# Rotary attention of a decoder's second layer: the product of the probabilities with the reciprocal sums moves from VectorE to GpSimd

## The chip, the cores and the metric

The kernel runs on one core of a Trainium2 chip. It is one program for a whole decoder of four layers (each with a self attention, a cross attention and a feed-forward part) on 32 sequences of 64 positions and width 128, all in fp32. The metric is the device time of one execution in microseconds, lower is better. The kernel before took 1555.16 us (median of 3 runs, 1553.07 to 1556.38).

In the profile's words PE is TensorE's matmul, PEld its weight load, DVE is VectorE, ACT is ScalarE, POOL is GpSimd and SP is SyncE.

## The reference

Only the self attention of layer 1 is touched. It has 16 heads of width 64, is causal, and turns queries and keys by a rotary table before their product:

```python
q, k = (apply_rope(q), apply_rope(k))
dots = jnp.einsum('bhid,bhjd->bhij', q, k) * scale
dots = jnp.where(causal, neg, dots)
attn = jax.nn.softmax(dots, axis=-1)
out = jnp.einsum('bhij,bhjd->bhid', attn, v)
out = out.transpose(0, 2, 1, 3).reshape(b, n, INNER)
out = jax.nn.relu(out @ W_o1) @ W_o2
```

After this comes a normalisation over the 128 features with a gain, and the sum is added to the stream `x`. The softmax's last step, the division by the row's sum of exponentials, is what the change moves.

## The kernel before

The 2048 tokens stand as 16 tiles of 128 rows (two sequences of 64). `rotary_attention` (from L1967) walks the tiles as a software pipeline that is written out by hand: each engine has its own loop over an index k, and in one turn of it works on several tiles at once, at different steps. The engines are tied by semaphores that count finished instructions, and each engine executes its own list strictly in order, so a wait holds back everything behind it.

Per tile t the steps are these.

- PE projects the queries into PSUM banks 0 and 1 and the keys into banks 2 and 3 (`project(t, 0)` and `project(t, 1)`, both L2018; the trace shows 16 matmul records for each), after the scores of tile t-1 have been read out of the same banks (`scored`, L2014).
- DVE multiplies each by the sine and the cosine table (`rotate`, L2205 and L2208). POOL adds the two products of the queries (L2192, two halves of 512), DVE those of the keys (L2217).
- PE multiplies queries and keys (`scores`, L2044).
- One turn later DVE adds the causal mask while it reads the scores from PSUM (`mask`, L2224), and finds the row maxima for the 16 heads (`find_max`, L2230 and L2232).
- ACT takes the exponentials head by head with their sums (`soften`, L2119; the sums land in `row_max`, 128x16).
- A further turn later DVE takes the reciprocals of the sums (L2238) and multiplies the 128x1024 probabilities by them, in place (L2240): the two instructions of `normalise`.
- PE turns the probabilities over (`turn_probs`, L2054), ACT copies them to SBUF (L2140), PE weighs the values (`weigh_values`, L2068), ACT copies the result (L2147), PE multiplies by the two output matrices (L2076 and L2083), with ACT's ReLU (L2151) and copy (L2127) between.
- DVE and POOL do the normalisations: statistics on DVE (L377, L380), the inverse root on POOL (`invert`, L387 and L389), and DVE applies it (L2256, L2259, L396).

PE's list in turn t is: `project(t,0)`, `turn_probs(t-2)`, `project(t,1)`, `weigh_values(t-2)`, half of the value projection of tile t+1 (L2031), `project_out(t-2)` (L2076), `scores(t)`, `project_mid(t-2)` (L2083), the other half of the value projection.

DVE's list in turn k is: `mask(k-1)`, `normalise(k-2)`, `find_max(k-1)`, `rotate(k,0)`, `rotate(k,1)`, the key sums, and then the normalisation steps of tiles k-4, k-5 and k-3.

POOL's list in turn k is: `invert` for tile k-5 and for tile k-4, then the query sums of tile k. In this stage POOL and SP issue no DMA inside the loop.

Of the kernel before, what the change touches and what calls it, by code (L numbers as in the profile page):

```python
# [13 lines left out]
ALU = mybir.AluOpType  # L14
# [5 lines left out]
B, S = 32, 64  # L20
NT = 16
# [178 lines left out]
def signals(core, names):  # L200


    words = names.split()
    turns = core.turns
    first = turns.taken
    turns.taken += len(words)
    return namedtuple("Signals", words)(*core.halves[turns.half][first:turns.taken])
# [112 lines left out]
def bcast(ap, dim, n):  # L320

    ap = ap.unsqueeze(dim)
    shape = list(ap.shape)
    shape[dim] = n
    return ap.to_broadcast(shape)
# [48 lines left out]
def measure(v, m, src, u, n=1):  # L374

    for t in range(u * n, u * n + n):
        v.bn_stats(m.stats_of[:, t], src[:, t]).then_inc(m.stats, 1)  # L377
    for t in range(u * n, u * n + n):
        v.wait_ge(m.stats, t + 1)
        v.bn_aggr(m.moments_of[:, t], m.stats_of[:, t]).then_inc(m.moments, 1)  # L380


def invert(c, g, m, u, n=1):

    own = slice(u * n, u * n + n)
    g.wait_ge(m.moments, u * n + n)
    g.tensor_scalar(m.var_eps_of[:, own], m.moments_of[:, own, 1], 1e-5, None, ALU.add).then_inc(m.var_eps, 1)  # L387
    g.wait_ge(m.var_eps, u + 1)
    g.tensor_tensor(m.rstd_of[:, own], m.var_eps_of[:, own], c.minus_half[:, 0:n], ALU.pow).then_inc(m.rstd, 1)  # L389


def scale(v, m, src, dst, u, n=1):

    v.wait_ge(m.rstd, u + 1)
    for t in range(u * n, u * n + n):
        v.tensor_scalar(dst[:, t], src[:, t], m.moments_of[:, t, 0:1], m.rstd_of[:, t:t + 1],  # L396
                        ALU.subtract, ALU.mult).then_inc(m.normed, 1)
# [1569 lines left out]
def rotary_attention(c):  # L1967
# [4 lines left out]
    s = signals(c, "turned_ps turned plain_ps by_cos by_sin q_rotated k_rotated v_ps v_ready scores_ps "  # L1972
                "scored max_ready bias_ready exp_ready inv_ready probs_ready probsT_ps "
                "probsT_ready o_ps o_ready mid_ps mid_ready y_ps y_ready weighted added")
# [8 lines left out]
    probs = lambda t: c.room(7 + t % 2)  # L1983
    probsT, outT = c.room(9), c.room(10)
    by_position = lambda a: a.rearrange("p (m k) -> p m k", k=S)
# [5 lines left out]
    @block.sync  # L1991
    def _(sp):

        for e in range(SLOTS["L1f"]):
            c.load_expert(sp, "L1f", e)
# [184 lines left out]
    @block.gpsimd  # L2180
    def _(g):
        invert_last(g)
        for k in range(NT + 6):
            if 0 <= k - 5 < NT:
                invert(c, g, following, k - 5)
            if 0 <= k - 4 < NT:
                invert(c, g, own, k - 4)
            if k < NT:
                g.wait_ge(s.by_sin, 2 * k + 1)
                for half in range(2):  # L2190
                    own_half = rotated[0][:, half * 512:(half + 1) * 512]
                    g.tensor_tensor(own_half, own_half, sines[0][:, (1 - half) * 512:(2 - half) * 512], ALU.add)\  # L2192
                        .then_inc(s.q_rotated, 1)

    @block.vector
    def _(v):
        def rotate(t, k):

            plain = c.ps[:, 2 * k:2 * k + 2].rearrange("p half n -> p (half n)")
            v.wait_ge(s.plain_ps, 2 * t + k + 1)  # L2200
            if t > 0:

                v.wait_ge((s.q_rotated, s.k_rotated)[k], 2 * t)
                v.wait_ge(s.scores_ps, t)
            v.tensor_tensor(by_half(sines[k]), by_half(plain),  # L2205
                            bcast(c.w("rope_sin").rearrange("p (half k) -> p half k", k=S), 2, CH), ALU.mult)\
                .then_inc(s.by_cos, 1)
            v.tensor_tensor(by_position(rotated[k]), by_position(plain), bcast(c.w("rope_cos"), 1, 2 * CH),  # L2208
                            ALU.mult).then_inc(s.by_sin, 1)

        def add_turned_keys(t):

            v.wait_ge(s.by_cos, 2 * t + 2)
            v.wait_ge(s.by_sin, 2 * t + 2)
            for half in range(2):
                own_half = rotated[1][:, half * 512:(half + 1) * 512]
                v.tensor_tensor(own_half, own_half, sines[1][:, (1 - half) * 512:(2 - half) * 512], ALU.add)\  # L2217
                    .then_inc(s.k_rotated, 1)

        def mask(t):  # L2220
            v.wait_ge(s.scores_ps, t + 1)
            if t >= 2:
                v.wait_ge(s.probsT_ps, 2 * (t - 1))
            v.tensor_tensor(by_bank(probs(t)), scores_ps, bcast(bcast(c.w("causal"), 1, 4), 1, 4),  # L2224
                            ALU.add).then_inc(s.scored, 1)

        def find_max(t):
            shaped = by_position(probs(t))
            v.wait_ge(s.scored, t + 1)
            v.tensor_reduce(c.row_max[:, t], shaped, AX.X, ALU.max).then_inc(s.max_ready, 1)  # L2230
            v.wait_ge(s.max_ready, t + 1)
            v.tensor_scalar(c.row_inv[:, t], c.row_max[:, t], -WH ** -0.5, None, ALU.mult)\  # L2232
                .then_inc(s.bias_ready, 1)

        def normalise(t):
            shaped = by_position(probs(t))
            v.wait_ge(s.exp_ready, t + 1)
            v.reciprocal(c.row_inv[:, t], c.row_max[:, t]).then_inc(s.inv_ready, 1)  # L2238
            v.wait_ge(s.inv_ready, t + 1)
            v.tensor_tensor(shaped, shaped, bcast(c.row_inv[:, t], 2, S), ALU.mult).then_inc(s.probs_ready, 1)  # L2240

        for k in range(NT + 6):
            if 0 <= k - 1 < NT:
                mask(k - 1)
            if 0 <= k - 2 < NT:
                normalise(k - 2)
            if 0 <= k - 1 < NT:
                find_max(k - 1)
            if k < NT:
                rotate(k, 0)  # L2250
                rotate(k, 1)
                add_turned_keys(k)
            t = k - 4
            if 0 <= t < NT:
                v.wait_ge(own.rstd, t + 1)
                v.scalar_tensor_tensor(out=c.hn[:, t], in0=c.att[:, t], scalar=own.moments_of[:, t, 0:1],  # L2256
                                       in1=c.w("L1_gamma"), op0=ALU.subtract, op1=ALU.mult).then_inc(s.weighted, 1)
                v.wait_ge(s.weighted, t + 1)
                v.scalar_tensor_tensor(out=c.x[:, t], in0=c.hn[:, t], scalar=own.rstd_of[:, t:t + 1],  # L2259
                                       in1=c.x[:, t], op0=ALU.mult, op1=ALU.add).then_inc(s.added, 1)  # L2260
                v.wait_ge(s.added, t + 1)
                measure(v, following, c.x, t)
            if 0 <= k - 5 < NT:
                scale(v, following, c.x, c.h, k - 5)
            if 0 <= k - 3 < NT:
                v.wait_ge(s.y_ready, k - 2)
                measure(v, own, c.att, k - 3)
# [624 lines left out]
```

## Time and profile before

| what | value |
|---|---|
| median of the runs | 1555.16 us |
| the profiled execution's own time | 1556.08 us |
| its span in the trace | 1554.2 us |
| the stage of this change, from its first matmul to its last normalised tile | about 319 to 550 us of the span |
| the 12 us from 429 to 441: PE, DVE, ACT, POOL busy | 11.82, 11.65, 9.10, 4.07 us |
| granted TensorE clock in that stretch | 1.00 (2.4 GHz) |

The span is one execution as the hardware profiler recorded it. Busy time of PE is modelled: matmuls are pipelined, and a busy PE may be one that runs at less than its peak. In a row of the timeline the first number is the start in us from the start of the span, the second the duration in us, then engine, line, operation, the output and the inputs, and in brackets how long the engine had stood idle before and whose work ended that.

### The profile page before, as it was taken

What the parts mean: (1) busy time and instruction counts of PE and PEld (TensorE: products, weight loads), DVE (VectorE), ACT (ScalarE), POOL (GpSimd) and SP (SyncE); (2) the same over time, 40 slices, a digit from 0 to 9 for tenths busy, and PEclk for the clock granted to TensorE, in tenths of its full rate; (3) what the DMA queues carried; (4) which work ended last, traced back from release to release, by engine and by line L of the source; (5) the groups of instructions that cost most, each with busy time, mean ns of one, the idle gap of its engine ahead of it and who ended that gap; (6) DMA issues with size and microseconds to landing.
All of it is one profiled execution on the core that took longest, in us unless ns stands there. A gap on an engine that the chain in (4) does not pass through costs nothing. (4 is left out here: it accounts for less than half of the span.)

```text
span 1554.2 us, 35844 instructions
## 1 busy us (share of the span) xinstructions
PE 1146.5 (74%) x14176; PEld 871.3 (56%) x14176; DVE 985.1 (63%) x2795; ACT 624.5 (40%) x1479; POOL 624.2 (40%) x700
## 2 busy tenths in 40 slices
PE   6864449759999779655688843189958876767988
PEld 3544449748888646554355743178844651554656
DVE  7977512188999658824567498333349957765762
ACT  4532224317777546112455321012214533643643
POOL 5655545422333245443224124723335634425430
PEclk9975579969999789667878665589977967867989
DMA  9900237450000095021000100345520000000000
GB/s 323 164 2 4 93 103 226 138 144 3 3 3 3 2 156 68 9 86 54 0 2 1 29 1 1 106 129 170 172 95 1 2 1 1 2 1 1 2 2 28
DMA packets 72730, 90.60 MB, mean 58 GB/s; under 512 B 5903, under 2 KB 59218, under 8 KB 71920
## 3 DMA queue, kind: packets, MB, share of 16 engines
q1 hardware_dynamic: 66544, 78.36, 20.1%
q0 software_dynamic: 6016, 9.93, 1.8%
q8 instruction: 113, 1.85, 0.5%
q14 instruction: 57, 0.47, 0.1%
HBM read 58.02 MB, written 32.69 MB: 58 GB/s over the span
## 5 line engine op out<-in xcount | busy, mean ns | idle before, releaser
L781 POOL TENSOR_TENSOR arena<-arena,small 128x1024 f32<-128x1024 f32 x80 | 155.4, 1947 | 98.8 <-ACT arena L663 61.6
L387 POOL TENSOR_SCALAR var_eps<-moments 128x1 f32<-128x1 f32 (+1 forms) x136 | 35.7, 262 | 326.2 <-DVE moments L380 326.1
L712 ACT ACTIVATE arena<-arena 128x1024 f32<-128x1024 f32 x80 | 84.7, 1059 | 93.7 <-DVE arena L860 93.7
L580 PE MATMUL ps<-arena,q 64*64 64x512 f32 x640 | 93.6, 652 | 21.8 <-POOL arena L781 18.5
L737 ACT COPY arena<-ps 128x512 f32<-128x512 f32 x160 | 86.3, 589 | 57.8 <-PE ps L590 57.5
L590 PEld LDWEIGHTS ps<-small,arena 128*128 128x128 f32 x640 | 74.0, 147 | 63.0 <-ACT arena L712 38.2
L1653 PEld LDWEIGHTS ps<-expert_ring,arena 128*128 128x128 f32 (+1 forms) x864 | 104.5, 192 | 2.9
L1653 PE MATMUL ps<-expert_ring,arena 128*128 128x128 f32 (+1 forms) x864 | 104.7, 275 | 0.0
L590 PE MATMUL ps<-small,arena 128*128 128x128 f32 x640 | 91.3, 288 | 12.6 <-ACT arena L712 12.6
L858 DVE TENSOR_REDUCE row_max<-ps 128x16 f32<-128x1024 f32 x48 | 58.7, 1223 | 64.7 <-PE ps L580 64.4
L389 POOL TENSOR_TENSOR rstd<-var_eps,minus_half 128x1 f32<-128x1 f32 (+1 forms) x136 | 89.6, 659 | 11.3
L602 PE MATMUL ps<-vx,arena 128*64 128x18 f32 x2560 | 93.9, 217 | 0.0
L602 PEld LDWEIGHTS ps<-vx,arena 128*64 128x64 f32 x2560 | 85.9, 144 | 14.1 <-issue 12.1
L2119 ACT ACTIVATE arena<-arena,row_inv 128x64 f32<-128x64 f32 x256 | 85.5, 341 | 0.0
L1634 PE MATMUL ps<-arena,expert_ring 128*112 128x256 f32 x368 | 84.4, 383 | 0.9 <-DMA expert_ring<-L2f_in 0.8
L1748 POOL DMA_INDIRECT home_L2f<-arena,home x46 | 44.7, 971 | 92.7 <-DVE arena L1914 69.1
L2192 POOL TENSOR_TENSOR arena<-arena 128x512 f32<-128x512 f32 x32 | 40.1, 1273 | 100.5 <-DVE arena L2208 100.5
L1705 ACT ACTIVATE arena<-ps 112x512 f32<-112x512 f32 x46 | 27.5, 597 | 126.4 <-PE ps L1634 126.4
L1621 PE MATMUL ps<-small,arena 128*128 128x128 f32 x108 | 22.4, 294 | 75.6 <-DMA arena<-slots_L2f 33.4
L1634 PEld LDWEIGHTS ps<-arena,expert_ring 128*112 128x112 f32 x368 | 64.2, 179 | 14.3 <-DMA expert_ring<-L2f_in 1.4
L396 DVE TENSOR_SCALAR h<-x,moments,rstd 128x128 f32<-128x128 f32 x192 | 66.7, 378 | 7.4 <-POOL rstd L389 7.4
L2018 PEld LDWEIGHTS ps<-hT,L_qkv 128*128 128x128 f32 x512 | 62.4, 199 | 13.9 <-DVE arena L2224 12.5
(363 smaller groups left out, 2861.6 us busy)
## 6 DMA issues: line engine op xcount, KB each, us to landing
expert_ring<-L2f_in SPq DMA_DIRECT2D x23, 704.0 KB, 4.4
expert_ring<-L0f_in SPq DMA_DIRECT2D x23, 578.0 KB, 4.1
slots_L0f<-blank SPq DMA_DIRECT2D x1, 8385.0 KB, 52.7
slots_L2f<-blank SPq DMA_DIRECT2D x1, 8385.0 KB, 51.0
small<-small_in SPq DMA_DIRECT2D x1, 4395.0 KB, 15.8
expert_ring<-L1f_in SPq DMA_DIRECT2D x8, 512.0 KB, 5.9
arena<-slots_L0f SPq DMA_DIRECT2D x23, 129.0 KB, 3.2
arena<-slots_L2f SPq DMA_DIRECT2D x23, 129.0 KB, 3.5
```

What stands on the lines that cost most here:

```text
L389: g.tensor_tensor(m.rstd_of[:, own], m.var_eps_of[:, own], c.minus_half[:, 0:n], ALU.pow).then_inc(m.rstd, 1)
L396: v.tensor_scalar(dst[:, t], src[:, t], m.moments_of[:, t, 0:1], m.rstd_of[:, t:t + 1], ALU.subtract, ALU.mult).then_inc(m.normed, 1)
L580: last = pe.matmul(c.ps[part(b), m], c.q[part(m), at:at + S], kx(t)[part(m), b * 512:(b + 1) * 512], start=not masked, stop=True)
L590: last = pe.transpose(c.ps[:, 2 + k, j * P:(j + 1) * P], buf(t)[:, (4 * k + j) * P:(4 * k + j + 1) * P], c.w("ident"))
L602: last = pe.matmul(o_ps(t)[part(b), j * 18:(j + 1) * 18], probsT(t)[:, seq(j, b)], c.vx[:, t % 8, b, j], start=True, stop=True)
L712: act.activation(buf(k), buf(k), ACT.Exp, scale=exp_scale).then_inc(s.probs_ready, 1)
L737: act.copy(probsT(t)[:, j * 512:(j + 1) * 512], c.ps[:, 2 + j])\
L781: g.tensor_tensor(kx(t).rearrange("p (b h k) -> p b h k", b=2, k=S), bcast(of_tile, 2, HEADS // 2), bcast(bcast(c.w("head_of_row"), 2, S), ...
L1634: last = pe.matmul(c.ps[0:width, 2 * (m % 2) + k, cols], ring(j)[:, k * hid + i * width:k * hid + (i + 1) * width], xT(j), start=True, sto ...
L1653: last = pe.matmul(c.ps[:, 4 + j % 2, tok(b)], hidden(j)[:, i, tok(b)], ring(j)[0:width, down_at + i * D:down_at + (i + 1) * D], start=(i ...
L2018: last = pe.matmul(c.ps[:, 2 * k + half, j * P:(j + 1) * P], w[:, at:at + P], c.hT[:, tok(t)], start=True, stop=True)
L2119: last = act.activation(probs(t)[:, g * S:(g + 1) * S], probs(t)[:, g * S:(g + 1) * S], ACT.Exp, bias=c.row_inv[:, t, g:g + 1], scale=WH * ...
```

## The change

The multiplication of the probabilities by the reciprocal sums becomes an instruction of POOL. It stands first in POOL's turn k, for tile k-2, ahead of the two `invert` and of the query sums, and it waits for the reciprocals of that tile (`inv_ready`). DVE keeps the reciprocal, at its old place behind the mask, and no longer waits for it. PE still waits for `probs_ready`, which POOL now counts up.

```diff
     def _(g):
         invert_last(g)
         for k in range(NT + 6):
+            if 0 <= k - 2 < NT:
+                shaped = by_position(probs(k - 2))
+                g.wait_ge(s.inv_ready, k - 1)
+                g.tensor_tensor(shaped, shaped, bcast(c.row_inv[:, k - 2], 2, S), ALU.mult).then_inc(s.probs_ready, 1)
             if 0 <= k - 5 < NT:
                 invert(c, g, following, k - 5)
             if 0 <= k - 4 < NT:
...
         def normalise(t):
-            shaped = by_position(probs(t))
             v.wait_ge(s.exp_ready, t + 1)
             v.reciprocal(c.row_inv[:, t], c.row_max[:, t]).then_inc(s.inv_ready, 1)
-            v.wait_ge(s.inv_ready, t + 1)
-            v.tensor_tensor(shaped, shaped, bcast(c.row_inv[:, t], 2, S), ALU.mult).then_inc(s.probs_ready, 1)
```

## Rows read from the trace of the kernel before

**Rows 1.** Busy time by stretch; columns: stretch, length, PE, PEld, DVE, ACT, POOL, clock, DMA.

```profile
429.00:441.00 12.00, 11.82 (x258) 9.79 (x257) 11.65 (x19) 9.10 (x40) 4.07 (x6) 1.00 0.01 3
...
525.00:540.00 15.00, 9.40 (x137) 8.16 (x130) 5.11 (x17) 7.74 (x36) 3.88 (x10) 0.61 0.00 1
```

**Rows 2.** Timeline of DVE, the masks of turns 3 and 4 of the loop.

```profile
364.94 1.23 DVE L2224 TENSOR_TENSOR arena<-ps,small 128x1024 f32<-128x1024 f32 x1 [2.11 <-PE ps L2044]
...
376.82 1.22 DVE L2224 TENSOR_TENSOR arena<-ps,small 128x1024 f32<-128x1024 f32 x1 [1.47 <-PE ps L2044]
```

**Rows 3.** Timeline of all engines, one turn of the loop in its steady state.

```profile
424.38 1.23 DVE L2224 TENSOR_TENSOR arena<-ps,small 128x1024 f32<-128x1024 f32 x1
...
424.60 0.19 ACT L2119 ACTIVATION_READ_ACCUMULATOR arena<-arena,row_inv 128x1 f32 x1
...
425.52 0.24 DVE L2238 RECIPROCAL row_inv<-row_max 128x16 f32<-128x16 f32 x1
...
425.66 1.86 PEld L2018 LDWEIGHTS ps<-hT,L_qkv 128*128 128x128 f32 x16 [0.87 <-DVE arena L2224]
...
425.80 1.22 DVE L2240 TENSOR_TENSOR arena<-arena,row_inv 128x1024 f32<-128x1024 f32 x1
...
427.55 1.04 PE L2054 MATMUL ps<-small,arena 128*128 128x128 f32 x8
...
428.42 1.95 PE L2018 MATMUL ps<-hT,L_qkv 128*128 128x128 f32 x16
...
429.44 1.22 DVE L2208 TENSOR_TENSOR arena<-ps,small 128x1024 f32<-128x1024 f32 x1
...
430.30 1.16 PE L2068 MATMUL ps<-arena 64*64 64x64 f32 x64
...
430.57 1.22 DVE L2205 TENSOR_TENSOR arena<-ps,small 128x1024 f32<-128x1024 f32 x1
...
430.73 2.51 POOL L2192 TENSOR_TENSOR arena<-arena 128x512 f32<-128x512 f32 x2 [5.23 <-DVE arena L2208]
...
432.66 1.86 PEld L2076 LDWEIGHTS ps<-arena,small 128*128 128x128 f32 x16 [0.97 <-ACT arena L2147]
...
434.64 1.59 PE L2044 MATMUL ps<-arena 32*64 32x64 f32 x128
...
436.27 1.23 DVE L2224 TENSOR_TENSOR arena<-ps,small 128x1024 f32<-128x1024 f32 x1
```

**Rows 4.** Instructions of one line: duration ns min/median/max, first and last start, forms.

```profile
L2240 DVE TENSOR_TENSOR arena<-arena,row_inv x16: 1224/1224/1227, 353.9 to 533.4; 128x1024 f32<-128x1024 f32 x16
...
L781 POOL TENSOR_TENSOR arena<-arena,small x80: 1893/1902/3447, 13.5 to 1484.1; 128x1024 f32<-128x1024 f32 x80
...
L2192 POOL TENSOR_TENSOR arena<-arena x32: 1264/1272/1281, 331.3 to 515.4; 128x512 f32<-128x512 f32 x32
```

**Rows 5.** Timeline of all engines, turn 2 and the end of the stage.

```profile
353.67 0.24 DVE L2238 RECIPROCAL row_inv<-row_max 128x16 f32<-128x16 f32 x1
...
356.21 1.04 PE L2054 MATMUL ps<-small,arena 128*128 128x128 f32 x8
...
520.88 0.24 DVE L2238 RECIPROCAL row_inv<-row_max 128x16 f32<-128x16 f32 x1
521.15 1.22 DVE L2240 TENSOR_TENSOR arena<-arena,row_inv 128x1024 f32<-128x1024 f32 x1
...
522.52 1.06 PE L2054 MATMUL ps<-small,arena 128*128 128x128 f32 x8 [2.41 <-DVE arena L2240]
...
534.81 1.94 PE L2054 MATMUL ps<-small,arena 128*128 128x128 f32 x8 [2.79 <-DVE arena L2240]
...
537.70 0.35 DVE L2256 SCALAR_TENSOR_TENSOR hn<-att,moments,small 128x128 f32<-128x128 f32 x1 [1.19 <-POOL rstd L389]
...
545.66 0.29 DVE L377 BATCH_NORM_STATS2 stats<-att 128x6 f32<-128x128 f32 x1 [6.44 <-ACT att L2127]
```

## The prediction, made before the changed kernel was run

> **What bounds the kernel now.** The change touches one stage, so the first view is the busy time by stretch, to see whether the engine that is relieved is the one that sets the pace. In its steady state DVE is busy 11.65 us of 12 and PE 11.82, at a granted clock of 1.00, the level of 2.4 GHz; ACT has 9.10 and POOL 4.07 [rows 1]. DVE looks full, but so does PE, and a share can't tell which of two full engines waits for the other. The second view is therefore the timeline of DVE at the loop's beginning, where the normalisation steps at the end of DVE's turn are not yet there. There the mask of turn 3 starts at 364.94 after DVE has stood idle for 2.11 us, waiting for PE's scores, and the next mask at 376.82 after 1.47 us idle [rows 2]. The turn takes 11.88 us. In the steady state the masks start at 424.38 and 436.27, 11.89 us apart [rows 3]. The pace is the same with 2 us of slack on DVE as with none: PE's chain sets it, and DVE fits into it.
>
> The third view, the timeline of one turn, shows that chain [rows 3]. The mask starts at 424.38 and its end lets `project(t,0)` go at 425.66 (PE had waited 0.87 us for it); `turn_probs` follows at 427.55 without a wait, `project(t,1)` at 428.42, `weigh_values` at 430.30, a value projection, then 0.97 us of waiting for ACT's copy, `project_out` at 432.66, `scores` at 434.64, and with their end the next mask at 436.27. There is no slack in it except what PE itself waits for, and these waits are links of the chain. The old multiplication is not a link: it ends at 425.80 + 1.22 = 427.02, half a microsecond before PE wants its product at 427.55.
>
> **The change part by part.**
>
> *DVE loses the multiplication.* From its start to that of the next instruction this is 1.14 us a tile; without the wait for the reciprocal perhaps 0.1 us more. By the first paragraph it buys nothing: the mask can't start before the scores. I take 0. Its upper bound, if DVE did set the pace, is a rival below. DVE also can't run ahead by 1.2 us: the query rotation would now meet PE's `project(t,0)`, which ends about 427.7, and the key rotation `project(t,1)`, which ends at 428.42 + 1.95 = 430.37, where it started at 430.57 before [rows 3]. So it keeps 0.2 us of lead, which it needs below.
>
> *POOL gains it: when it starts.* The reciprocal keeps its place behind the mask, and the exponentials it needs are there before (the last sum is out at 424.79), so it still ends at 425.52 + 0.24 = 425.76. POOL stands idle then. It took 0.07 us from the end of DVE's L2208 (429.44 + 1.22) to its own start at 430.73, so the multiplication starts about 425.84 [rows 3].
>
> *How long it takes.* POOL does not have this instruction in the trace. The same instruction on DVE, 1.22 us, is the lower end. The nearest POOL row is L781: 128x1024, a multiplication, one operand repeated along the inner dimension just like the reciprocals here, 1.90 us at its median over 80 of them (the longest, 3.45, stands far from a minimum and a median that lie together, and I leave it out). The other near row is L2192 in this very stage, in place like the new one, but 512 wide and with two full operands: 1.27 us, so two of them 2.54 us, the upper end [rows 4]. I take 1.90, since size, operation and broadcast agree, and keep 1.22 and 2.54 for the range.
>
> *What PE waits.* PE's first transpose began 0.15 us after the multiplication's end where it did wait for it (521.15 + 1.22 = 522.37, then 522.52) [rows 5]. So it now begins at 425.84 + 1.90 + 0.15 = 427.89 in place of 427.55: 0.34 us late. With 1.22 us there is no delay (427.21), with 2.54 it is 0.98. The eight transposes, `project(t,1)`, `weigh_values`, `project_out`, `scores` and the next mask stand behind them on PE's list or wait for them, and ACT's copies and exponentials too. No wait in between gets shorter: PE's 0.97 us for ACT starts from `weigh_values` and shifts with it. The reciprocal is tied to the mask, so the delay does not feed itself; each turn becomes 11.89 + 0.34 = 12.23 us.
>
> The Trainium skill, GPSIMD Engine Reference, section 3.1, says that an elementwise instruction with two inputs on GpSimd can take at best one element in about 2.5 cycles of its 1.2 GHz, since both inputs come through one read port. By that an estimate for this one is 1024 x 2.5 / 1.2 = 2.13 us. L781 with 1.90 us is faster than the rule and L2192 with 2.54 us a pair slower [rows 4]. By the rule the delay would be 0.57 us a turn, and the sum made below 9.3 us.
>
> *How many turns.* `turn_probs` runs in turns 2 to 17. In turn 2 PE was still late by itself: the reciprocal ends at 353.91, POOL would be through at 355.89, and PE's transposes began at 356.21, so nothing is lost [rows 5]. Turns 3 to 15 repeat the pattern: 13 x 0.34 = 4.4 us. In turns 16 and 17 there is no projection ahead of the transposes, and PE waited for the multiplication itself (2.41 and 2.79 us idle) [rows 5]; there all of the difference counts: POOL starts at 520.88 + 0.24 + 0.08 = 521.20 in place of DVE's 521.15, and takes 0.68 us longer, 0.73 us each, 1.5 us for both. With 2.54 us of multiplication it is 1.37 each.
>
> *The clock at the end.* After turn 15 PE has long idle stretches, and the granted clock from 525 to 540 us is 0.61 on average, between the two levels. The transposes of turn 16 took 1.06 us, those of turn 17 took 1.94 [rows 1, 5]. If those of turn 16, now 0.7 us later, fall to the lower level, they cost 0.9 us more. I take 0.3.
>
> *POOL's other work moves behind the multiplication.* In the steady turn POOL is through with it at 427.74, the two `invert` need some 1.7 us and end near 429.5, and the query sums can start when DVE's L2208 ends, which is 430.66 before and not earlier than about 430.1 after [rows 3]. POOL's turn then still holds free time, so I count nothing. If POOL took 2.54 us, the `invert` would end at 430.1, still in time. In turn 17 the multiplication waits for the last exponentials, and the `invert` of tiles 12 and 13 wait behind it: DVE's L2256 work there comes some 2.5 to 3 us later than before (that of the next turn started at 537.70). But DVE then idles 6.44 us until 545.66, for PE's last tile [rows 5]; this hides it. Without that cover it would cost the 3 us. No DMA stands in POOL's list here, and SP's is untouched.
>
> *Sum.* 4.4 + 1.5 + 0.3 = 6.2 us more. The profiled execution's own time is 1556.08 us (its span of 1554.2 and 1.9 around it), 0.92 above the median of the runs. So the profiled time would become 1562.3, and the median 1561.4. The lower end of the terms is 0.1 (a multiplication as fast as DVE's), giving 1555.3; the upper end is 13 x 0.98 + 2.7 + 0.9 = 16.3, giving 1571.5.
>
> **The rivals.**
>
> *POOL takes 2.5 us.* For it: L2192 is in place and in this stage. Against it: its operands are both full. Result 1555.16 + 16 = about 1571; between this and the forecast every length is possible, and some of these lie near 1566.
>
> *The delay is hidden.* PE's transposes would have to find their data by 427.55, with a multiplication of at most 1.55 us. For it: only DVE's 1.22. Against it: none of POOL's 80 L781 was under 1.893 [rows 4]. Then only the last two turns lose, 0.1 to 0.8 us: 1555.5, no change.
>
> *DVE sets the pace after all, and the kernel gets faster.* The place is the mask at 424.38 and 436.27, which show no idle time in front of them [rows 3]. If in these turns it was DVE's own list and not the scores that held the mask, every turn from 5 on would shrink by up to 1.2 us until PE binds: 14 x 1.2 = 17 us, 1538. It decides only if DVE comes to the mask later than the scores do; but turns 3 and 4, with 2.11 and 1.47 us of wait, have the same length to 0.01 us [rows 2], which leaves it no room.
>
> *The added wait costs the clock.* PE stands still once more in each turn. If the grant fell to the lower level, the transposes would take 1.94 us for 1.04 [rows 3, 5], and a turn with some 10 us of PE work up to 8 us more: 100 us over 13 turns, 1655. Against it: two waits of 0.87 and 0.97 us a turn left the clock at 1.00.
>
> **How the numbers follow.** The forecast has 0.60, with a range of its own of 1559 to 1564.5 (a multiplication of 1.8 to 2.1 us). POOL slower than that has 0.21. Hidden has 0.13, faster through DVE 0.04, the clock 0.02. A measurement of this kernel tells a change from none at about 0.2%, 3.1 us, so slower begins at 1558.3: the forecast, POOL slower and the clock make 0.82 with a little taken off for runs that scatter; no change 0.14; faster 0.04. The range leaves the clock, the rival through DVE and the tails of the others out: 1556.5 to 1570.
>
> **What the profile after would show.** POOL should have 16 new multiplications near 1.90 us that start some 0.08 us behind the reciprocals; PE's L2054 should wait for them, about 0.4 us in each of turns 3 to 15, where it waited for nothing; masks should stand 12.2 us apart, with DVE idle in front of them or of the key rotation; ACT's busy time and the clock should be as before. I am wrong if the masks come less than 11.89 us apart, if L2054 still starts without a wait, or if L2192 becomes the wait in front of the scores.

## The result, and the profile after

The changed kernel is slower: 1563.4 us against 1560.48 (medians of 20 runs each; the runs of the kernel before had a median of 1555.16 when there were three of them). The ratio is 1.0045, with a 95% interval of 1.0026 to 1.0065, some 7 us (4 to 10); the forecast was 1.0040, or 6.2 us. This ratio is not the quotient of the two medians, which lie only 2.9 us apart (the means 4.6), so the whole time shows that the change costs something, but the amount only roughly. The profiled execution of after took 1563.27 us, with a span of 1561.5 us, 7.3 more than before.

Single executions of this program scatter by several us whatever the kernel, so the stage itself, in the profiled execution of each kernel, is the better measure. From its first matmul (L2008) to the first matmul of the next stage (L517) it lasts 231.2 us before and 238.7 after: 7.5 us, and the rest of the program differs by 0.2. Of these 7.5 us, 0.8 lie in the beginning of the stage and are not the change's, as is shown further down.

First the busy times of one turn of the changed kernel, from mask to mask, and of the stage's end; columns as in [rows 1]:

```profile
417.62:429.88 12.26, 11.91 (x255) 9.71 (x255) 11.05 (x17) 9.00 (x41) 5.93 (x7) 1.00 0.01 3
525.00:540.00 15.00, 10.00 (x230) 9.06 (x229) 7.68 (x20) 9.34 (x46) 3.42 (x5) 0.73 0.01 2
```

The turn has grown from 11.89 to 12.26 us with the clock at 1.00 as before. DVE is busy for less of it than [rows 1] showed, POOL for more, and nothing got faster. The second window covers another part of the tail than before, so its clock can't be set beside the 0.61 there.

The timeline of that turn shows why; it answers to [rows 3], and the lines of DVE and POOL are numbered anew (L2228 is the mask, L2241 the reciprocal, L2187 POOL's product, L2236 the scaled maxima, L2209 and L2212 the rotation, L2196 the query sums):

```profile
417.62 1.23 DVE L2228 TENSOR_TENSOR arena<-ps,small 128x1024 f32<-128x1024 f32 x1 [0.26 <-PE ps L2044]
...
418.77 0.24 DVE L2241 RECIPROCAL row_inv<-row_max 128x16 f32<-128x16 f32 x1
...
419.09 1.90 POOL L2187 TENSOR_TENSOR arena<-arena,row_inv 128x1024 f32<-128x1024 f32 x1 [5.41 <-DVE row_inv L2241]
420.14 0.88 DVE L2236 TENSOR_SCALAR row_inv<-row_max 128x16 f32<-128x16 f32 x1
...
420.99 1.22 DVE L2209 TENSOR_TENSOR arena<-ps,small 128x1024 f32<-128x1024 f32 x1
...
421.13 1.06 PE L2054 MATMUL ps<-small,arena 128*128 128x128 f32 x8 [0.18 <-POOL arena L2187]
...
422.04 1.95 PE L2018 MATMUL ps<-hT,L_qkv 128*128 128x128 f32 x16
...
423.43 2.51 POOL L2196 TENSOR_TENSOR arena<-arena 128x512 f32<-128x512 f32 x2 [0.75 <-DVE arena L2212]
...
424.02 1.22 DVE L2209 TENSOR_TENSOR arena<-ps,small 128x1024 f32<-128x1024 f32 x1 [0.67 <-PE ps L2018]
...
426.27 1.86 PEld L2076 LDWEIGHTS ps<-arena,small 128*128 128x128 f32 x16 [0.96 <-ACT arena L2147]
...
428.25 1.59 PE L2044 MATMUL ps<-arena 32*64 32x64 f32 x128
...
429.88 1.22 DVE L2228 TENSOR_TENSOR arena<-ps,small 128x1024 f32<-128x1024 f32 x1 [0.26 <-PE ps L2044]
```

PE's transposes begin 421.13 - 417.62 = 3.51 us after the mask, where [rows 3] have 427.55 - 424.38 = 3.17: 0.34 us late. They now name POOL as what they waited for; the row has only 0.18 us of idle time, since the L2018 before them is counted as busy until 420.95 and the transposes of [rows 3] had started 0.16 us before that point of the turn. Behind them every step has its old distance, PE's 0.96 us for ACT too. DVE, with an instruction less, now waits for PE twice a turn, 0.67 us for the projected keys and 0.26 us in front of the mask.

The end of the stage, which answers to [rows 5]:

```profile
529.39 1.90 POOL L2187 TENSOR_TENSOR arena<-arena,row_inv 128x1024 f32<-128x1024 f32 x1 [5.41 <-DVE row_inv L2241]
531.43 1.45 PE L2054 MATMUL ps<-small,arena 128*128 128x128 f32 x8 [3.13 <-POOL arena L2187]
...
533.56 1.99 PE L2068 MATMUL ps<-arena 64*64 64x64 f32 x64 [0.68 <-ACT arena L2140]
...
544.89 1.94 PE L2054 MATMUL ps<-small,arena 128*128 128x128 f32 x8 [3.21 <-POOL arena L2187]
...
546.47 0.35 DVE L2257 SCALAR_TENSOR_TENSOR hn<-att,moments,small 128x128 f32<-128x128 f32 x1 [3.70 <-POOL rstd L389]
...
555.97 0.29 DVE L377 BATCH_NORM_STATS2 stats<-att 128x6 f32<-128x128 f32 x1 [4.85 <-ACT att L2127]
```

PE's idle time before L2054 went from 2.41 to 3.13 us in turn 16 and from 2.79 to 3.21 in turn 17. The transposes of turn 16 now took 1.45 us for 1.06, so part of them ran at the lower clock (0.68 granted on average from 531.43 to 532.90). In the kernel before, the clock fell a step later, behind the transposes:

```profile
524.31 1.89 PE L2068 MATMUL ps<-arena 64*64 64x64 f32 x64 [0.73 <-ACT arena L2140]
...
527.38 3.78 PE L2076 MATMUL ps<-arena,small 128*128 128x128 f32 x16 [1.18 <-ACT arena L2147]
```

### The profile page after: what moved, and what is told of

Read it like the earlier page. It is cut to its first block and busy times, and to the rows that moved or that the text cites. A ratio compares the mean times of both kernels' runs of the same rounds, so it can differ in the third digit from the quotient of the medians.

```text
span 1561.5 us, 35844 instructions
## 1 busy us (share of the span) xinstructions
PE 1145.3 (73%) x14176; PEld 870.3 (56%) x14176; DVE 976.1 (63%) x2779; ACT 625.3 (40%) x1479; POOL 652.1 (42%) x716
## 5 line engine op out<-in xcount | busy, mean ns | idle before, releaser
L781 POOL TENSOR_TENSOR arena<-arena,small 128x1024 f32<-128x1024 f32 x80 | 154.6, 1936 | 102.9 <-ACT arena L663 64.6
L2018 PEld LDWEIGHTS ps<-hT,L_qkv 128*128 128x128 f32 x512 | 62.0, 197 | 14.2 <-DVE arena L2228 12.7
L1712 ACT ACTIVATE arena<-ps,expert_ring 128x256 f32<-128x256 f32 x92 | 38.6, 471 | 75.6 <-PE ps L1642 75.1
```

Of the source, the lines that this page charges most:

```text
L781: g.tensor_tensor(kx(t).rearrange("p (b h k) -> p b h k", b=2, k=S), bcast(of_tile, 2, HEADS // 2), bcast(bcast(c.w("head_of_row"), 2, S), ...
L2018: last = pe.matmul(c.ps[:, 2 * k + half, j * P:(j + 1) * P], w[:, at:at + P], c.hT[:, tok(t)], start=True, stop=True)
```

## The experiments

The theory: PE's chain from mask to mask sets the turn, and the change costs exactly what POOL's product is late for PE's transposes, plus twice the difference at the end. Its rivals: DVE sets the pace; DVE's L2236, held up from 0.17 to 0.88 us beside POOL's product, is the cost; the work queued behind the product on POOL is the cost. Stage, turn and end below are differences of starts in each kernel's trace (turn: between the masks of turns 4 to 15; end: from the mask of turn 16 to L517; "mask moved": that mask itself starts later by the edit, so this end can't be set beside the others). Turn, stage and end are from one profiled execution each.

| kernel | turn us | stage us | end us | ratio to before, 95% interval |
|---|---|---|---|---|
| before | 11.89 | 231.2 | 30.4 | 1 |
| after | 12.26 | 238.7 | 32.5 | 1.0045 [1.0026, 1.0065] |
| e1_no_product | 11.89 | 222.7 | 24.4 | 1.1869 [1.1819, 1.1919] |
| e2_split_keys | 12.04 | 235.5 | 32.7 | 1.0027 [0.9999, 1.0055] |
| e3_bias_on_act | 12.26 | 238.7 | 32.6 | 1.0104 [1.006, 1.0147] |
| e4_invert_first | 12.26 | 239.0 | 32.5 | 1.0035 [1.0008, 1.0062] |
| e5_two_halves, e5_timed | 11.90 | 229.0, 232.5 | 30.5, 31.4 | 0.9989 [0.9958, 1.002] |
| e6_product_twice | 14.24, four of 15.8 | 275.6 | 36.3 | one run |
| e8_split_keys_four | 11.89 | 233.5 | 32.1 | 0.9971 [0.994, 1.0001] |
| e9_last_first | 11.89 | 228.1 | 27.3, mask moved | 0.9991 [0.9961, 1.0021] |
| e10_early_copy | 12.25 | 237.0 | 32.6 | 1.0038 [1.0002, 1.0075] |
| e11_last_first | 11.90 | 228.5 | 29.4, mask moved | 0.998 [0.9944, 1.0016] |
| e12_all | 12.25 | 237.2 | 31.4, mask moved | 1.0016 [0.9983, 1.0049] |

The stage's first 45 us, before the steady turns, took 43.8 us in one execution of e5's code and 46.3 in the other (in all kernels the first mask comes 18.5 or about 20 us after the start, in before and after 20.0 and 20.4), so stages are compared by turn and by end. The end varies too: e5's two executions have 30.5 and 31.4 us. In the first, half of the transposes of turn 16 took 0.63 us, in the second all of them 2.02, after the same wait:

```profile
524.39 0.63 PE L2054 MATMUL ps<-small,arena 128*128 128x128 f32 x4 [2.27 <-POOL arena L2188]
```

```profile
532.51 2.02 PE L2054 MATMUL ps<-small,arena 128*128 128x128 f32 x8 [2.27 <-POOL arena L2188]
```

The same code met the lower clock at different places, so a difference of about 1 us between two ends says nothing about an edit.

**e1: the product left out, on the kernel before.**

```diff
-            shaped = by_position(probs(t))
             v.wait_ge(s.exp_ready, t + 1)
-            v.reciprocal(c.row_inv[:, t], c.row_max[:, t]).then_inc(s.inv_ready, 1)
-            v.wait_ge(s.inv_ready, t + 1)
-            v.tensor_tensor(shaped, shaped, bcast(c.row_inv[:, t], 2, S), ALU.mult).then_inc(s.probs_ready, 1)
+            v.reciprocal(c.row_inv[:, t], c.row_max[:, t]).then_inc(s.probs_ready, 1)
```

> Left out: the product of the probabilities with the reciprocals (neither VectorE nor GpSimd does it); the rest is the kernel before. Theory (PE's chain from mask to mask sets the turn, DVE has slack): the masks of turns 5 to 15 stay 11.89 us apart, with DVE idle in front of them, and only turns 16 and 17, where PE waits for the product itself, gain about 1.2 us each: some 2.5 us less than before, -0.15%. Rival (DVE sets the pace): each turn from 5 on is 1.1 to 1.2 us shorter, some 15 to 17 us less, -1%.

A turn of its timeline from mask to mask, and the end:

```profile
438.54 1.23 DVE L2224 TENSOR_TENSOR arena<-ps,small 128x1024 f32<-128x1024 f32 x1 [0.26 <-PE ps L2044]
...
450.43 1.22 DVE L2224 TENSOR_TENSOR arena<-ps,small 128x1024 f32<-128x1024 f32 x1 [0.26 <-PE ps L2044]
...
523.29 1.06 PE L2054 MATMUL ps<-small,arena 128*128 128x128 f32 x8 [1.15 <-DVE row_inv L2237]
...
525.09 1.16 PE L2068 MATMUL ps<-arena 64*64 64x64 f32 x64 [0.73 <-ACT arena L2140]
...
527.69 2.05 PE L2076 MATMUL ps<-arena,small 128*128 128x128 f32 x16 [1.44 <-ACT arena L2147]
```

The turn is still 11.89 us, with a whole instruction of 1.22 us gone from DVE and DVE now idle in front of each mask. So DVE does not set the pace, and moving its work wins next to nothing there. It had hardly any time to spare, though. In one of the 13 turns of the kernel before, DVE paused for 0.28 us, PE's scores waited for DVE's key sums, and the turn took 12.12 us:

```profile
452.43 1.22 DVE L2205 TENSOR_TENSOR arena<-ps,small 128x1024 f32<-128x1024 f32 x1 [0.28 <-issue]
...
458.66 1.58 PE L2044 MATMUL ps<-arena 32*64 32x64 f32 x128 [0.17 <-DVE arena L2217]
```

e9, where DVE has the product too, has such a turn as well; e1 has none. The end won 6.0 us where 2.5 were expected: with 1.15 us idle before L2054 in place of 2.41, L2068 took 1.16 and L2076 2.05 us, the durations of the steady turns, while before the change they were at 1.89 and 3.78 there. How much of these 6.0 us is the product's and how much a clock that fell later, one execution can't tell. The 290 us more of the whole program lie elsewhere: other values reach the sparse attention of layer 3, and it goes into a sort (L1307, 576 instructions on DVE, from 1319.9 to 1607.4 us) that the kernel before never runs.

**e6: POOL's product done twice, on the changed kernel.**

```diff
-            pe.wait_ge(s.probs_ready, t + 1)
+            pe.wait_ge(s.probs_ready, 2 * t + 2)
...
-                g.tensor_tensor(shaped, shaped, bcast(c.row_inv[:, k - 2], 2, S), ALU.mult).then_inc(s.probs_ready, 1)
+                for turn in range(2):
+                    g.wait_ge(s.probs_ready, 2 * (k - 2) + turn)
+                    g.tensor_tensor(shaped, shaped, bcast(c.row_inv[:, k - 2], 2, S), ALU.mult)\
+                        .then_inc(s.probs_ready, 1)
```

> The changed kernel with POOL's product done twice in place (so the probabilities are divided twice; all else is as it was). Theory (each turn is as much longer as the product comes late for PE): POOL is 1.90 + 0.05 us later, masks 12.26 + 1.95 = 14.2 us apart, PE waits some 2.3 us in front of L2054 in each turn of the steady state; the stage 13 x 1.95 + 2 x 1.95 + up to 2 for the clock, 29 to 33 us longer than in the changed kernel (238.7 us). Rival (POOL's product is beside the path and the cost lies elsewhere, in DVE's held-up L2236 or in the order of POOL's work): the masks grow by well under 1.95 us.

```profile
403.76 0.71 PE L2054 MATMUL ps<-small,arena 128*128 128x128 f32 x5
...
404.31 3.57 PE L2018 MATMUL ps<-hT,L_qkv 128*128 128x128 f32 x16
...
419.26 1.06 PE L2054 MATMUL ps<-small,arena 128*128 128x128 f32 x8 [2.16 <-POOL arena L2189]
420.16 1.95 PE L2018 MATMUL ps<-hT,L_qkv 128*128 128x128 f32 x16
...
429.48 3.88 POOL L2189 TENSOR_TENSOR arena<-arena,row_inv 128x1024 f32<-128x1024 f32 x2 [6.18 <-DVE row_inv L2244]
430.52 0.88 DVE L2239 TENSOR_SCALAR row_inv<-row_max 128x16 f32<-128x16 f32 x1
```

The two products take 3.88 us and the turn grows by 1.98: a microsecond of POOL's product is a microsecond of the turn. Four of the 13 turns are 15.82 to 15.85 us long instead of 14.24. In one of them L2018 behind the wait took 3.57 us for 1.95, in the other three 3.39 to 3.53: the clock went to its lower level there (0.51 granted over the first 2 us of the 3.57, 1.00 over the transposes just before). The rival of the prediction in which the added wait costs the clock is thus real, though only with 2.16 us of waiting a turn, not with 0.18. The sort ran here too, so the whole time says nothing about the product.

**e3 and e4: the two other suspects, on the changed kernel.** In e3 the scaling of the maxima leaves DVE, in e4 POOL's two inverse roots stand ahead of the product:

```diff
+            if 0 <= k - 1 < NT:
+                act.wait_ge(s.max_ready, k)
+                act.activation(c.row_inv[:, k - 1], c.row_max[:, k - 1], ACT.Copy, scale=-WH ** -0.5)\
+                    .then_inc(s.bias_ready, 1)
...
-            v.wait_ge(s.max_ready, t + 1)
-            v.tensor_scalar(c.row_inv[:, t], c.row_max[:, t], -WH ** -0.5, None, ALU.mult)\
-                .then_inc(s.bias_ready, 1)
```

> The changed kernel, but the small product of the row maxima with the scale (L2236, 128x16, 0.17 us before and 0.88 us after the change) is done by ScalarE ahead of its copies of the turned probabilities, where ScalarE waits anyway. Rival (the hold-up of L2236 on DVE beside POOL's product is the cost): masks go back from 12.26 towards 11.9 us and the time by some 4.6 us towards the kernel before. Theory (PE's wait for the product): masks stay at 12.26 us, +7 us on the kernel before; DVE merely waits 0.7 us for the query projection in its place.

> The changed kernel, but POOL's two inverse roots of a turn stand ahead of the product, so that neither they nor anything behind them waits for the last exponentials. Rival (work queued behind the product on POOL is the cost): masks back towards 11.9 us or the end of the stage shorter by 2 us or more. Theory: masks stay at 12.26 us and the end of the stage as long as in the changed kernel (within 0.3 us), since the inverse roots are done before the reciprocal and DVE's late L2257 in the last turns was hidden; +7 us on the kernel before.

e3, one turn:

```profile
431.65 1.91 POOL L2191 TENSOR_TENSOR arena<-arena,row_inv 128x1024 f32<-128x1024 f32 x1 [5.41 <-DVE row_inv L2242]
432.70 0.22 ACT L2167 ACTIVATE row_inv<-row_max 128x16 f32<-128x16 f32 x1 [0.22 <-DVE row_max L2238]
...
433.56 1.22 DVE L2213 TENSOR_TENSOR arena<-ps,small 128x1024 f32<-128x1024 f32 x1 [0.89 <-PE ps L2018]
...
433.70 1.06 PE L2054 MATMUL ps<-small,arena 128*128 128x128 f32 x8 [0.18 <-POOL arena L2191]
```

The turn stays at 12.26 us in both. In e3 DVE waits 0.89 us for the projected queries where it was held up for the product, and starts the rotation at the same distance from the mask. Its ratio of 1.0104 rests on four runs and is larger than its stage explains; where the rest lies is open. In e4 the end is as long as after the change (32.5 us), although DVE's L2257 no longer waits 1.69 and 3.70 us there: that wait was hidden, as the prediction had it.

**e2 and e8: PE is given other work ahead of the transposes, on the changed kernel.** `project` takes the halves to do as a further argument:

```diff
                 project(t, 0)
+                project(t, 1, (0,))
             if t >= 2:
                 turn_probs(t - 2)
             if t < NT:
-                project(t, 1)
+                project(t, 1, (1,))
```

> The changed kernel, but half of the key projection (8 of its 16 matmul records, 0.94 us) stands ahead of the transposes on PE's list and half behind. Theory (the changed kernel's loss is PE's wait in front of the transposes): the wait vanishes, since the transposes are then due 0.94 us later and the product is 0.37 us late; masks 11.89 to 12.0 us apart against 12.26 in the changed kernel; the stage keeps only the 2 us at its end and 0.4 in turn 2, so about +2.5 us on the kernel before, +0.15%. Rivals (the loss is in DVE's L2236 held up to 0.88 us, or in POOL's other work queued behind the product): both are still there, masks stay at 12.26, +7 us.

> e2 (half of the key projection ahead of the transposes) with one more edit: ScalarE takes four exponentials and not five between its copies of the turned probabilities and its copies of the weighed values. Theory: the 0.15 us a turn that e2 kept (12.04 against 11.89) came from ScalarE, which got to L2149 0.2 us after PE's values were there; with four it is there in time, masks 11.89 to 11.92 us apart, the stage some 2 us shorter than e2's 235.5 us. If something else in the moved product costs the 0.15 us, masks stay at 12.04.

e2:

```profile
433.52 1.04 PE L2055 MATMUL ps<-small,arena 128*128 128x128 f32 x8
...
435.38 1.16 PE L2069 MATMUL ps<-arena 64*64 64x64 f32 x64
...
436.79 1.05 ACT L2149 COPY arena<-ps 128x512 f32<-128x512 f32 x2
...
437.89 1.86 PEld L2077 LDWEIGHTS ps<-arena,small 128*128 128x128 f32 x16 [1.12 <-ACT arena L2149]
```

The transposes (L2055 here) no longer wait. e2 missed its range of 11.89 to 12.0 by a little, with 12.04 us: ACT reached its copies (L2149) late, since its five exponentials began behind the later copies of the turned probabilities. With four exponentials ahead of them (e8: `range(5)` becomes `range(4)`) the turn is 11.89 us. The whole product stands on POOL in e8 and costs nothing in the turns; only the end, at 32.1 us, keeps it.

**e5: POOL's product in two halves of eight heads, on the changed kernel.**

```diff
-            pe.wait_ge(s.probs_ready, t + 1)
             for k in range(2):
+                pe.wait_ge(s.probs_ready, 2 * t + k + 1)
...
-                g.tensor_tensor(shaped, shaped, bcast(c.row_inv[:, k - 2], 2, S), ALU.mult).then_inc(s.probs_ready, 1)
+                for half in (slice(0, 8), slice(8, 16)):
+                    g.tensor_tensor(shaped[:, half], shaped[:, half], bcast(c.row_inv[:, k - 2, half], 2, S),
+                                    ALU.mult).then_inc(s.probs_ready, 1)
```

> The changed kernel with POOL's product in two instructions of eight heads, and PE's first four transposes waiting for the first only. Theory: the first half is there before PE wants it, the second ends 2.2 to 2.55 us after POOL's start (1.09 us each like the shortest 512-wide rows, or 1.27 like L2192), and only four transposes (0.43 us) stand behind it: masks 12.1 us apart with the short halves, 12.4 with the long ones, against 12.26.

```profile
426.51 1.22 DVE L2230 TENSOR_TENSOR arena<-ps,small 128x1024 f32<-128x1024 f32 x1 [0.26 <-PE ps L2044]
...
427.97 2.04 POOL L2188 TENSOR_TENSOR arena<-arena,row_inv 128x512 f32<-128x512 f32 x2 [4.98 <-DVE row_inv L2243]
429.68 1.05 PE L2054 MATMUL ps<-small,arena 128*128 128x128 f32 x8
```

Both halves together take 2.04 us, less than either length that was expected. The first is out long before PE asks for it; the second ends at 430.01, when PE is still at the first four transposes. The turn is 11.90 us.

> e5 once more, now timed. Its trace had masks 11.90 us apart, PE's transposes unhindered and a stage of 229.0 us (231.2 before, 238.7 after the change). Theory: the whole cost of the change was the latency of one 1024-wide product, and in two halves the kernel is as fast as before to within 0.2% (-2 us to +1 us); the rival is that something of the 7 us outside this wait stays, then +3 us or more.

Timed, it is the kernel before to within what can be told: the interval runs from 6.5 us faster to 3.1 slower, which leaves out the 7 us of the change, but hardly a rest of 3 us.

**e9 to e12: beyond the kernel before.**

> The kernel before (product on VectorE), with one edit: in turn 16, the first without a projection ahead of the transposes, VectorE does the reciprocal and the product of tile 14 ahead of the mask of tile 15. PE's idle time before L2054 falls from 2.41 us to about 1.75. Theory A (the granted clock falls in the tail because PE stands idle too long there; in e1, with 1.15 us idle, L2068 and L2076 of that turn kept 1.16 and 2.05 us for 1.89 and 3.78): the turn's L2068 and L2076 go back to 1.16 and 2.05 us, the stage is 3 to 4 us shorter than 231.2 us, -0.2%. Theory B (the clock falls anyway by then): only the 0.67 us of the earlier product are won, and part of that is lost again by the later mask: 0 to 0.7 us, no change.

> e5 with PE's weighing of the values done one sequence after the other, so that ScalarE copies the first bank while PE fills the second, and PE's 0.97 us of waiting in front of L2076 is shortened. If the weighing keeps its 1.16 us, PE's chain gets up to 0.4 us shorter and the masks come 11.5 to 11.65 us apart (DVE's 0.26 us of idle time in front of the mask is then used up), some 4 us less than before. If the weighing needs the alternation of the two row halves for its speed, L2068 takes 1.6 us or more and the turn is not shorter, or longer: 11.9 to 12.8 us.

> e5 with two edits in turn 16: VectorE takes the reciprocal of tile 14 ahead of the mask of tile 15, and ScalarE copies the weighed values of tile 14 ahead of the exponentials of tile 15. In e9 the first edit alone left L2068 at 1.16 us but let PE wait 2.30 us for ScalarE, and L2076 took 3.20 us. Theory (what PE's clock loses at the end comes from its idle times there): with both, L2076 of that turn takes 2.05 us and the stage is 2 to 3.5 us shorter than e5's 229.0 us. If the clock falls anyway: 0 to 1 us shorter.

> e10 and e11 together, the candidate to beat both kernels: turns as in e10, the end of the stage as in e11. If both hold, some 6 to 7 us less than the kernel before, -0.4%; if only the end holds, 2 to 3 us less, which the timing can hardly tell from nothing; slower if the weighing in e10 slows down.

```diff
+            if k == NT:
+                normalise(k - 2)
             if 0 <= k - 1 < NT:
                 mask(k - 1)
-            if 0 <= k - 2 < NT:
+            if 0 <= k - 2 < NT and k != NT:
                 normalise(k - 2)
```

That is e9's edit; e11 has it on e5, with ScalarE's `take_weighed(14)` ahead of its exponentials in the same turn; e10 is e5 with the loop over the two sequences outermost in `weigh_values` and a count of `o_ps` for each. PE in the end of e9, in a turn of e10, and in the end of e11:

```profile
524.87 1.06 PE L2054 MATMUL ps<-small,arena 128*128 128x128 f32 x8 [1.72 <-DVE arena L2240]
...
526.66 1.16 PE L2068 MATMUL ps<-arena 64*64 64x64 f32 x64 [0.72 <-ACT arena L2140]
...
530.12 3.20 PE L2076 MATMUL ps<-arena,small 128*128 128x128 f32 x16 [2.30 <-ACT arena L2147]
```

```profile
432.48 1.91 PE L2068 MATMUL ps<-arena 64*64 64x64 f32 x64
...
435.07 1.96 PEld L2076 LDWEIGHTS ps<-arena,small 128*128 128x128 f32 x16 [0.46 <-ACT arena L2147]
```

```profile
526.38 0.63 PE L2054 MATMUL ps<-small,arena 128*128 128x128 f32 x4 [1.57 <-POOL arena L2190]
...
528.62 1.84 PE L2068 MATMUL ps<-arena 64*64 64x64 f32 x64 [0.68 <-ACT arena L2140]
```

e9 got L2068 back to 1.16 us, but not L2076, and from the mask of turn 15 on it has 1.2 us less (41.0 against 42.3), hardly more than the 0.9 us between the two executions of e5. In e11 L2068 was slow in spite of a shorter wait for its transposes (1.57 us), against what theory A expected, and its stage is 0.5 us shorter than e5's 229.0, as its expectation has it if the clock falls anyway. When exactly the clock falls at the end is open. e10's loop order costs more than its earlier copy wins: L2068 went from 1.16 to 1.91 us, while PE's wait for ACT fell from 0.97 to 0.46. e12 inherits that. None of the four can be told from the kernel before as faster.

## Why the prediction was right

- *What bounds.* PE's chain, not DVE. e1 took 1.22 us from DVE and the turn stayed 11.89 us. The price put on DVE's relief, nothing, was right but for 0.23 us: the one turn of 12.12 us in which DVE held PE up is gone.
- *Start and length of POOL's product.* Forecast 0.08 us behind the reciprocal and 1.90 us long; measured 419.09 - (418.77 + 0.24) = 0.08, and 1.899 to 1.904 us in all 16. The row that agreed in size, operation and broadcast (L781, [rows 4]) was the right one to take. The pair of L2192, with two full operands, was too long; by it the turn would have been 12.87 us against the measured 12.26. The Trainium skill's 2.5 cycles an element (GPSIMD Engine Reference, section 2.1; section 3.1, which the prediction names, has 2.6) give the estimate of 2.13 us, which was too long as well: a turn of 12.46 us.
- *PE's wait.* Forecast 0.34 us late and 12.23 us a turn; measured 0.34 and 12.26. Most of the rest is in L2054 itself: from its start to the next L2018 it is 0.91 us after a wait and was 0.87 without [rows 3]. Over 13 turns the masks of turns 3 to 16 lie 159.4 us apart against 154.8, 4.6 us more; forecast 4.4. That is 13 x 0.37 = 4.8 us less the 0.23 of the turn of 12.12 us.
- *Turn 2* was counted at nothing, and took 12.85 us for 12.41. The product did not make it longer. It came late there, since the reciprocal waited 0.28 us for the exponentials, but POOL was through at 359.44 and PE's transposes began at 359.84 without a wait: PE was late by itself, as the prediction has it. The clock did it: in turn 2 it was granted 0.95 on average before and 0.92 after, and PE's value projection, which stands ahead of the transposes, took 1.71 us after the change for 1.27 before, which is the whole 0.44. Other kernels agree: turn 2 took 12.1 us at 0.97 (e1, e5), 12.9 at 0.91 (e4, e8) and 13.6 at 0.86 (e5 when timed). After, and the projection before:

```profile
356.51 1.71 PE L2031 MATMUL ps<-L_qkv,hT 128*128 128x512 f32 x2
...
357.54 1.90 POOL L2187 TENSOR_TENSOR arena<-arena,row_inv 128x1024 f32<-128x1024 f32 x1 [5.12 <-DVE row_inv L2241]
...
359.84 1.04 PE L2054 MATMUL ps<-small,arena 128*128 128x128 f32 x8
```

```profile
353.33 1.27 PE L2031 MATMUL ps<-L_qkv,hT 128*128 128x512 f32 x2
```

- *The end.* Forecast 2 x 0.73 us and 0.3 for the clock; measured 0.72 in each turn (L2054 3.51 us behind the mask for 2.79, and 8.15 us behind L2076 for 7.43) and some 0.7 us for slower matmuls, in all 32.5 against 30.4 us: 2.1 for 1.8. The 0.72 are the product's; the 0.7 for the clock are less than e5's two executions differ by, so that this term came out near is in part luck.
- *POOL's other work and DVE's late L2257* were counted at nothing, and e4 shows that they cost nothing: without that wait its end is 32.5 us as well.
- *Not foreseen:* DVE's L2236 beside POOL's product, 0.88 us for 0.17. e3 shows that it cost nothing either, since DVE would have waited for PE's projection at that place.

The sum of the parts in the trace is 4.6 + 2.1 + 0.8 at the beginning = 7.5 us, the stage's difference. Of the 0.8, 0.4 stand ahead of the first product and 0.4 in turn 2, so the change itself costs 6.7 us there, against 6.2 forecast.

The forecast as a time, 1561.4 us, lies near the measured 1563.4 partly by luck: the median of the kernel before, on which it was built, had risen from 1555.16 to 1560.48 us in the longer series. The forecast rests on the turn and the end, and these came out as it had them.

Two sums of the prediction are off, and neither bears on the forecast. By the rule cited there from the Trainium skill the sum is 13 x 0.57 + 2 x 0.96 + 0.3 = 9.6 us; 9.3 leaves out the clock's 0.3. And the turns from 5 to 17, for the rival in which DVE sets the pace, are 13, not 14: 15.6 us.

## What to carry to other kernels

A busy share near 97% does not make an engine the bound: look for a stretch in which it has less to do and see whether the pace changes. An instruction that moves to an idle but slower engine is priced by when its consumer wants its result, not by the engine's free time; here 0.38 us of slack was there (half a microsecond, less the 0.15 us from the end of the product to PE's start), and an instruction that ended 0.72 us later used it up. Cutting such an instruction in two, so that its consumer can start on the first half, took back the turns' loss where a whole one was 0.34 us late.

## What the runs showed of the hardware

- POOL's product of 128x512 with a broadcast operand took 1.04 us (1039 to 1045 ns, 32 of them in e5) and that of 128x1024 1.90 us; halving it cost 0.14 us in all.
- DVE's 16-column L2236, 0.17 us by itself in e1 and before, took 0.88 us beside POOL's product and ended with it (420.14 + 0.88 = 421.02; the product at 420.99). With two products in a row (e6) it still took 0.88 and ended with the first, so it got in between them. The maximum over 1024 columns just before ran beside the same product at 1.18 us. The Trainium skill, SBUF — State Buffer, section "SBUF: two separate sides", says that VectorE, in its two-port modes, and GpSimd lock one pair of ports for a whole instruction; this hold-up agrees, though no run here shows in which mode L2236 was.
- PE's weighing of the values, 64 records on 64 x 64 parts, took 1.16 us with the row halves in alternation and 1.91 us with one half after the other (e10).
